# A four-layer network on one core: the pseudo-inverse recurrence with symmetric operands, and another opening of the first attention stage

## The chip, the cores and the metric

The kernel runs on one core of a Trainium2 chip. The metric is the device time of one execution in microseconds (us); lower is better. One execution is also taken by the hardware profiler, and its page and trace are what is read here. TensorE has two clock levels, 1.2 and 2.4 GHz; the profile gives the granted clock as 0.50 and 1.00 of full speed.

## The reference

The network takes x of 8 images, 16 x 16 positions and 192 channels, and applies in order: a window attention with relative positions (windows of 14 x 14, 12 heads of 16) and its MLP, a Fourier filter, a landmark attention, a mixture of experts (two of eight), a full attention and a mixture of experts (one of eight). Two places matter here. The first is the window attention:

```python
attn = jnp.einsum('bqc,bkc->bqk', q * scale, k)
attn = (attn.reshape(-1, WS, WS, WS, WS) + rel_h[:, :, :, :, None] + rel_w[:, :, :, None, :]).reshape(-1, N, N)
attn = jax.nn.softmax(attn, axis=-1)
out = attn @ v
```

The second is the pseudo-inverse in the landmark attention, on one 16 x 16 matrix per image and head:

```python
v = (1.0 / jnp.max(jnp.sum(k_mat, axis=-2), axis=-1))[:, None, None] * jnp.swapaxes(k_mat, -1, -2)
for _ in range(6):
    kv = k_mat @ v
    v = 0.25 * v @ (13.0 * I - kv @ (15.0 * I - kv @ (7.0 * I - kv)))
```

Here kv starts as K times its own transpose (times a number), which is symmetric, and each step of the recurrence is a polynomial in it.

## The kernel before

`build` (L2852) runs the layers as stages, each with its own programs for the engines: TensorE (PE), VectorE (DVE), ScalarE (ACT), GpSimd (POOL), and SyncE (SP), which issues most DMAs. An engine runs its program in order; the engines meet at semaphores. The prefix of a tile names its stage: l0a is the window attention, l2i the pseudo-inverse, l3a the full attention.

**Window attention, `window_attention` (L961).** The work is 12 groups k (pairs of images times groups of four heads), each of three parts j (two windows, then the border), each of four heads s: 36 steps n of four items, 144 items. For an item `score` (L1071) multiplies four times into one of two banks psS, and VectorE takes the maxima (`maxima`, L1267), so that the item after next waits for `max_done`. The maxima of a group are split in three bf16 pieces by POOL, turned by TensorE (`turn_max`), copied by ACT and sent by DMA as three more rows of QS. Only then can `score_t` (L1111) form the transposed scores, ACT take their exponentials (`exps`) and TensorE multiply with the values (`values`). `steps` (L1000) starts at n = -lead = -6: the scores run six steps, 24 items, ahead of the transposed scores. For these first 24 items TensorE does `score` alone, with one `turn_max` among them.

The inputs of a group lie in a ring of four slots. SP's `load` (L1019) issues 13 DMAs for a slot: RS from rd (one, 336 KB), QS from qd (six of 64 KB) and KS from kd (six of 64 KB, by `term_rows`, L954); `stack_in` of the slot counts all 13. ACT's queue first issues six small DMAs to kb (L1208), then the four window rows of RS (L1210), KOH (L1211) and Wo (L1212). VectorE waits for kb and spreads it into KP (L1264) before its first maxima. TensorE opens with six products of 512 columns on data that is there (L1184), each of them two records in the trace since the operands are f32; their result is overwritten. Then it waits for `pads_done` (KP) and all five constants on `c_in`, and in the first `score` for `stack_in`.

**Pseudo-inverse, `l2_inverse` (L1851).** Sixteen block-diagonal matrices of 96 x 96 are kept as [96, 16, 96]. A `product` (L1879) is 16 f32 matmuls (32 records), four to a PSUM bank, four banks; `done` rises once per bank. K2 is turned by TensorE and copied to K2T by ACT (L1915); VectorE scales K2 to VT (L1952) and K2T to Vm (L1954), bank by bank in turn. A loop of six iterations on each engine then does six products: A = K V (to D7 by VectorE, L1960), the transpose of A (to AT by ACT, L1919), A D7 (to D15), A D15 (to D13), V D13 (to Vm by VectorE, L1969) and its transpose (to VT by ACT, L1922). A last product with K3 gives MB. That makes 6 x 6 + 1 = 37 products. The products alternate between the banks ps0 to ps3 and ps4 to ps7.

Of the kernel before, what the change touches and what calls it, by code (L numbers as in the profile page):

```python
# [9 lines left out]
ALU = mybir.AluOpType  # L10
ACT = mybir.ActivationFunctionType
# [9 lines left out]
CH = C // 2  # L21
# [13 lines left out]
K_TERM = (0, 1, 2, 0, 1, 0)  # L35
# [161 lines left out]
KS = 33  # L197
# [763 lines left out]
def window_attention(nc, G, w_out, stats_eps):  # L961
# [7 lines left out]
    with Stage(nc, "l0a") as st:  # L969
# [27 lines left out]
        c_in, kb_in, pads_done, zeroed, x_biased = st.sems("c_in kb_in pads_done zeroed x_biased")  # L997
# [20 lines left out]
        def _(sp):  # L1018
            def load(k):  # L1019
# [6 lines left out]
                term_rows(sp, KS[slot], G["kd"], at, K_TERM, stack_in[slot])  # L1026
# [824 lines left out]
def l2_inverse(nc, G, consts):  # L1851


    with Stage(nc, "l2i") as st:
# [5 lines left out]
        K2, K2T, AT, D7, D15, D13, Vm, VT = (big(n) for n in ("K2", "K2T", "AT", "D7", "D15", "D13", "Vm", "VT"))  # L1860
        ps = [st.ps(f"ps{b}") for b in range(8)]
        c_in, sm, exp_done, col_mm, col_done, bd_done, k2t_mm, k2t_done, start_done = st.sems("c_in sm exp_done col_mm col_done bd_done k2t_mm k2t_done start_done")
        a_mm, at_mm, at_done, d7_done, b_mm, d15_done, c_mm, d13_done, v_mm, vt_mm, v_done, vt_done = st.sems(
            "a_mm at_mm at_done d7_done b_mm d15_done c_mm d13_done v_mm vt_mm v_done vt_done")
# [6 lines left out]
        ITERATIONS = 6  # L1871

# [6 lines left out]
        def product(pe, b0, lhs, rhs, gate, gate_at, done):  # L1879

            for b in range(NBK):
                for s, at in zip(gate, gate_at):
                    pe.wait_ge(s, at + b)
                for g in range(b * GB, (b + 1) * GB):
                    mm = nc.tensor.matmul(ps[b0 + b][0:CH, (g % GB) * CH:(g % GB + 1) * CH], lhs[:, g, :], rhs[:, g, :], start=True, stop=True)  # L1885
                mm.then_inc(done, 1)

        @block.tensor
        def _(pe):
            pe.wait_ge(c_in, 48)  # L1890
# [8 lines left out]
            with pe.Fori(0, ITERATIONS) as it:  # L1899

                product(pe, 0, K2T, Vm, (v_done, vt_done), (4 * it + 1, 4 * it + 1), a_mm)
                product(pe, 4, Vm, K2T, (vt_done,), (4 * it + 1,), at_mm)
                product(pe, 0, AT, D7, (at_done, d7_done), (4 * it + 1, 4 * it + 1), b_mm)
                product(pe, 4, AT, D15, (d15_done,), (4 * it + 1,), c_mm)
                product(pe, 0, VT, D13, (d13_done,), (4 * it + 1,), v_mm)
                product(pe, 4, D13, VT, (d13_done,), (4 * it + 1,), vt_mm)
            product(pe, 0, VT, K3, (v_done, vt_done), (4 * ITERATIONS + 1, 4 * ITERATIONS + 1), mb_mm)

        @block.scalar
        def _(act):  # L1910
# [5 lines left out]
            with act.Fori(0, ITERATIONS) as it:  # L1916
                for b in range(NBK):
                    act.wait_ge(at_mm, 4 * it + b + 1)
# [963 lines left out]
```

## Time and profile before

| | us |
|---|---|
| median of 3 runs | 1607.22 |
| lowest, highest of them | 1604.24, 1630.35 |
| profiled execution, its time | 1617.94 |
| profiled execution, its span | 1616.1 |
| mean granted clock in it | 0.823 |

The span reaches from the first to the last instruction; the execution's own time is 1.8 us longer. The window attention takes from 157.2 us to about 380 us of the span, the pseudo-inverse from 758.7 to 870.7 us. In the views, a group of rows gives the start and the length in us, the engine, the line and the tiles (out <- in); "PEld" is TensorE's weight load, which overlaps its matmuls; a bracket at the end of a row tells how long the engine sat idle before it and what released it.

### The profile page before, as it was taken

The numbers are of one execution on the slowest core, as the hardware profiler recorded it, in microseconds if no ns is written. First come the engines' busy times: TensorE is split into PE (matmuls) and PEld (weight loads), VectorE is DVE, ScalarE is ACT, GpSimd is POOL, SyncE is SP. The second block draws the span as 40 slices with busy tenths as digits, with TensorE's granted clock in tenths as the row PEclk, the third lists the DMA queues.
The fourth block names the chain that finished last, engine by engine and source line by source line (L and its number), as shares of the span: only waits on it lengthen the run. The fifth ranks groups of instructions, "written<-read, shape, count | busy, mean of one in ns | idle before, by whom it ended". The sixth has DMA issues, their size and how long they took to land. (4 is left out here: it accounts for less than half of the span.)

```text
span 1616.1 us, 25003 instructions
## 1 busy us (share of the span) xinstructions
PE 1212.6 (75%) x8342; PEld 968.3 (60%) x8343; DVE 604.4 (37%) x1430; ACT 468.9 (29%) x947; POOL 302.0 (19%) x513
## 2 busy tenths in 40 slices
PE   1866899996986786888997564699945679961892
PEld 0765677884974565766997453466634435541782
DVE  2333433542103654434554340233335557522011
ACT  0633133553422231333211023111103336620330
POOL 3224300112000111000001306100036531114003
PEclk9975556997996997987998756799978789965896
DMA  4223522311111001000000055111112243141453
GB/s 87 59 67 108 109 58 58 87 31 33 39 61 42 0 0 38 1 0 4 1 0 6 14 147 163 47 48 46 47 53 67 79 136 95 42 106 39 118 141 88
DMA packets 123405, 95.53 MB, mean 59 GB/s; under 512 B 33298, under 2 KB 114508, under 8 KB 123212
## 3 DMA queue, kind: packets, MB, share of 16 engines
q1 hardware_dynamic: 108648, 83.13, 19.2%
q0 software_dynamic: 4608, 9.44, 2.2%
q10 hardware_dynamic: 10084, 2.11, 0.8%
q8 instruction: 38, 0.62, 0.2%
q14 instruction: 27, 0.22, 0.0%
HBM read 67.21 MB, written 35.20 MB: 63 GB/s over the span
## 5 line engine op out<-in xcount | busy, mean ns | idle before, releaser
L2402 PE MATMUL l2e_psH<-W1T,l2e_XT 96*128 x160 | 79.2, 618 | 10.1 <-issue 5.3
L1273 DVE TENSOR_REDUCE l0a_nmax<-l0a_psS 98x2 f32<-98x392 f32 x96 | 54.2, 566 | 65.8 <-PE l0a_psS L1083 63.5
L913 DVE TENSOR_REDUCE l3a_nmax<-l3a_psS 128x2 f32<-128x512 f32 x96 | 62.3, 686 | 40.0 <-PE l3a_psS L764 40.0
L1221 ACT ACTIVATE l0a_PT<-l0a_psST 98x392 f32<-98x392 f32 x96 | 47.2, 497 | 68.0 <-PE l0a_psST L1125 67.7
L869 ACT ACTIVATE l3a_PT<-l3a_psST 128x512 f32<-128x512 f32 x96 | 54.7, 596 | 31.7 <-PE l3a_psST L794 31.2
L2435 ACT ACTIVATE l2e_H<-l2e_psH 128x512 f32<-128x512 f32 x40 | 23.9, 597 | 137.3 <-PE l2e_psH L2402 137.3
L1082 PE MATMUL l0a_psS<-l0a_KS,l0a_QS 96*98 96x196 bf16 x192 | 55.2, 319 | 5.5 <-DMA l0a_KS<-kd 5.4
L2418 PE MATMUL l2e_psY<-W2T,l2e_HT 128*128 x320 | 58.5, 326 | 0.0
L2451 DVE COPY l2e_HT<-l2e_psT 128x512 f32<-128x512 f32 x40 | 27.6, 691 | 76.5 <-PE l2e_psT L2410 76.5
L1083 PE MATMUL l0a_psS<-l0a_KOH,l0a_RS 90*98 90x196 bf16 x192 | 53.4, 309 | 0.0
L2418 PEld LDWEIGHTS l2e_psY<-W2T,l2e_HT 128*128 128x128 f32 x320 | 51.1, 190 | 0.0
L1960 DVE SCALAR_TENSOR_TENSOR l2i_D<-l2i_ps,l2i_eyes 96x384 f32<-96x384 f32 x72 | 39.9, 554 | 26.8 <-PE l2i_ps L1885 19.2
L618 PE MATMUL l0r_ps<-QF,l0r_Rbd 96*84 x256 | 39.3, 327 | 14.0 <-DVE l0r_Rbd L642 14.0
L1124 PE MATMUL l0a_psST<-l0a_QS,l0a_KS 99*98 99x196 bf16 x192 | 49.3, 291 | 0.2 <-ACT l0a_PT L1221 0.2
L1125 PE MATMUL l0a_psST<-l0a_RS,l0a_KOH 90*98 90x196 bf16 x192 | 48.9, 288 | 0.0
L2402 PEld LDWEIGHTS l2e_psH<-W1T,l2e_XT 96*128 96x128 f32 x160 | 27.9, 194 | 34.7 <-issue 34.7
L2574 PE MATMUL l3e_psH<-l3e_XT,expert_W 96*128 96x256 f32 x192 | 44.8, 395 | 4.0 <-DMA expert_b<-in_L_ffn_b 2.7
L618 PEld LDWEIGHTS l0r_ps<-QF,l0r_Rbd 96*84 96x84 f32 x256 | 39.2, 238 | 14.3 <-issue 14.3
L161 PE MATMUL l3p_psT<-ident,l3p_xn 128*96 128x128 f32 x32 | 8.0, 425 | 50.1 <-DVE l3p_xn L151 50.1
L1378 PE MATMUL l0m_psH<-l0m_xT,l0m_W 96*128 96x256 f32 x192 | 44.7, 395 | 0.4 <-ACT l0m_xT L173 0.4
L2574 PEld LDWEIGHTS l3e_psH<-l3e_XT,expert_W 96*128 96x128 f32 x192 | 37.8, 199 | 10.7 <-issue 5.2
L1082 PEld LDWEIGHTS l0a_psS<-l0a_KS,l0a_QS 96*98 96x98 bf16 x192 | 30.1, 157 | 22.8 <-issue 9.9
(485 smaller groups left out, 2979.4 us busy)
## 6 DMA issues: line engine op xcount, KB each, us to landing
expert_W<-in_L_ffn_w SPq DMA_DIRECT2D x16, 576.0 KB, 4.3
l2r_raw<-in_L_ffn_w SPq DMA_DIRECT2D x16, 384.0 KB, 4.5
l0a_QS<-qd SPq DMA_DIRECT2D x72, 64.0 KB
l0a_KS<-kd SPq DMA_DIRECT2D x72, 64.0 KB
l3a_QS<-qd SPq DMA_DIRECT2D x72, 64.0 KB, 2.3
l3a_KS<-kd SPq DMA_DIRECT2D x72, 64.0 KB, 2.3
rd<-l0r_r_p SPq DMA_DIRECT2D x24, 168.0 KB
l0a_RS<-rd SPq DMA_DIRECT2D x12, 336.0 KB
```

The source lines that it names most:

```text
L618: mm = nc.tensor.matmul(ps[bank][0:HB * WS, col + k * B * cnt:col + (k + 1) * B * cnt], Rbd[:, axis, i0 + k, :], free(src, [2 * T, B // 2] ...
L869: nc.scalar.activation(PT[n % 3][:, s, :], psST[item % 2][:, :], ACT.Exp).then_inc(exp_done, 1)
L913: nc.vector.tensor_reduce(nmax[k % 2][:, TI * u:TI * (u + 1), s], psS[item % 2][:, :].rearrange("p (t k) -> p t k", t=TI), AX.X, ALU.max, ...
L1082: nc.tensor.matmul(o, q_[:, s, q], k_[:, s, keys], start=True, stop=False)
L1083: mm = nc.tensor.matmul(o, r_[:, s, q], KOH[:, keys], start=False, stop=True)
L1124: nc.tensor.matmul(o, k_[:, s, keys], q_[:, s, q], start=True, stop=False)
L1125: mm = nc.tensor.matmul(o, KOH[:, keys], r_[:, s, q], start=False, stop=True)
L1221: ex = nc.scalar.activation(PT[n % 3][0:WQ, s, :], psST[item % 2][0:WQ, 0:2 * W0], ACT.Exp)
L1273: mx = nc.vector.tensor_reduce(nmax[k % 2][0:WQ, 2 * j:2 * (j + 1), s], psS[item % 2][0:WQ, 0:2 * W0].rearrange("p (t k) -> p t k", t=2), ...
L2402: mm = nc.tensor.matmul(psH[b][:, :], XT[b][:, k, :], G["W1T"][:, k, bass.ds(e * FI, FI)], start=(k == 0), stop=(k == 1))
L2418: mm = nc.tensor.matmul(psY[b][:, 0:C], HT[b][:, mb, :], G["W2T"][:, bass.ds(e * NM + mb, 1), :].rearrange("p a c -> p (a c)"), start=(mb ...
L2574: mm = nc.tensor.matmul(psH[k2][:, m % 2 * CAP:(m % 2 + 1) * CAP], W1[b][:, k, m * P:(m + 1) * P], XT[b][:, k, :], start=(k == 0), stop=(k ...
```

## The change

In the pseudo-inverse, the transposed product of A is dropped: since A is symmetric, A itself is used as the stationary operand. A is kept by ACT (in place of AT), and VectorE makes D7 from this copy in SBUF instead of from PSUM. In iterations 0 to 3, A of the next iteration is formed as 0.25 A D13, so that V is not needed, and only VT is carried. Iteration 4 forms V D13 and K V anew; iteration 5 forms VT alone. The loops are written out. At the start VectorE makes all four banks of Vm first, then VT.

In the window attention, the opening has 20 products instead of 6. The six KS loads of slot 0 move from SP's queue to ACT's, where they follow the window rows of slot 0 and KOH and stand ahead of kb and the other three window rows. TensorE waits before the first score for the first two constants only (`c_in` 32); for the other window rows (`rest_in`) at k = 1, and for `pads_done` at the first border item (n = 2).

```diff
@@ window_attention
-                term_rows(sp, KS[slot], G["kd"], at, K_TERM, stack_in[slot])
+                if k:
+                    term_rows(sp, KS[slot], G["kd"], at, K_TERM, stack_in[slot])
...
                     pe.wait_ge(stack_in[k % ring], 13 * 16 * (k // ring + 1))
+                    if k == 1:
+                        pe.wait_ge(rest_in, 16 * (ring - 1))
+                if j == 2 and k == 0 and s == 0:
+                    pe.wait_ge(pads_done, 1)
...
-            for c in range(6):
+            for c in range(20):
                 nc.tensor.matmul(psS[0][:, :], G["ident"][0:CH, :], G["QF"][:, 0, c * W2 % (B * T):c * W2 % (B * T) + W2], start=True, stop=True)
-            pe.wait_ge(pads_done, 1)
-            pe.wait_ge(c_in, 16 * (ring + 1))
+            pe.wait_ge(c_in, 32)
...
+            act.dma_start(RS[0][RR:RM, :, :], rows(G["consts"]["winrows"], 0, [W2, RM - RR], [0, GQ], [1, W2])).then_inc(c_in, 16)
+            act.dma_start(KOH[:, :], G["consts"]["koh"]).then_inc(c_in, 16)
+            term_rows(act, KS[0], G["kd"], 0, K_TERM, stack_in[0])
             for t, piece in enumerate(K_TERM):
                 act.dma_start(kb[t * HD:(t + 1) * HD, :], rows(G["kbd"], piece * C, [1, HD], [HD, NH]), allow_slow_non_contiguous=True).then_inc(kb_in, 16)
-            for k in range(ring):
-                act.dma_start(RS[k][RR:RM, :, :], rows(G["consts"]["winrows"], 0, [W2, RM - RR], [0, GQ], [1, W2])).then_inc(c_in, 16)
-            act.dma_start(KOH[:, :], G["consts"]["koh"]).then_inc(c_in, 16)
+            for k in range(1, ring):
+                act.dma_start(RS[k][RR:RM, :, :], rows(G["consts"]["winrows"], 0, [W2, RM - RR], [0, GQ], [1, W2])).then_inc(rest_in, 16)
@@ l2_inverse, TensorE
-            with pe.Fori(0, ITERATIONS) as it:
-
-                product(pe, 0, K2T, Vm, (v_done, vt_done), (4 * it + 1, 4 * it + 1), a_mm)
-                product(pe, 4, Vm, K2T, (vt_done,), (4 * it + 1,), at_mm)
-                product(pe, 0, AT, D7, (at_done, d7_done), (4 * it + 1, 4 * it + 1), b_mm)
-                product(pe, 4, AT, D15, (d15_done,), (4 * it + 1,), c_mm)
-                product(pe, 0, VT, D13, (d13_done,), (4 * it + 1,), v_mm)
-                product(pe, 4, D13, VT, (d13_done,), (4 * it + 1,), vt_mm)
-            product(pe, 0, VT, K3, (v_done, vt_done), (4 * ITERATIONS + 1, 4 * ITERATIONS + 1), mb_mm)
+            LO, HI = 0, 4
+            product(LO, K2T, Vm, a_mm, (v_done, 0))
+            for it in range(ITERATIONS):
+                at = NBK * it
+                product(HI, A, D7, b_mm, (d7_done, at))
+                product(LO, A, D15, c_mm, (d15_done, at), (vt_done, at))
+                if it < LAST - 1:
+                    product(HI, A, D13, a_mm, (d13_done, at))
+                    product(LO, D13, VT, vt_mm, (d13_done, at))
+                elif it == LAST - 1:
+                    product(HI, VT, D13, v_mm, (d13_done, at))
+                    product(LO, D13, VT, vt_mm, (d13_done, at))
+                    product(HI, K2T, Vm, a_mm, (v_done, NBK))
+                else:
+                    product(HI, D13, VT, vt_mm, (d13_done, at))
+            product(LO, VT, K3, mb_mm, (vt_done, NBK * ITERATIONS))
@@ l2_inverse, ScalarE and VectorE
+            keep(A, 0, a_mm, a_done, 0, 1.0)
+            for it in range(ITERATIONS):
+                at = NBK * it
+                if it < LAST - 1:
+                    keep(A, 4, a_mm, a_done, at + NBK, 0.25)
+                keep(VT, 4 if it == LAST else 0, vt_mm, vt_done, at, 0.25)
+                if it == LAST - 1:
+                    keep(A, 4, a_mm, a_done, at + NBK, 1.0)
...
+                minus(D7, lambda b: A[:, gs(b), :], 0, a_done, at, d7_done)
+                minus(D15, lambda b: bank(4 + b), 2, b_mm, at, d15_done)
+                minus(D13, bank, 1, c_mm, at, d13_done)
+                if it == LAST - 1:
+                    for b in range(NBK):
+                        dve.wait_ge(v_mm, b + 1)
+                        nc.vector.tensor_scalar(Vm[:, gs(b), :], bank(4 + b), 0.25, None, ALU.mult).then_inc(v_done, 1)
```

`keep` is four ACT copies, one per bank, each waiting for its bank of the product and raising `done`; `minus` is four VectorE operations of the same kind.

## Rows read from the trace of the kernel before

**Rows 1.** The page: TensorE's granted clock in 40 slices of the span, in tenths
```profile
PEclk9975556997996997987998756799978789965896
```

**Rows 2.** Timeline of the pseudo-inverse, one full iteration
```profile
785.57 2.80 PEld L1885 LDWEIGHTS l2i_ps<-l2i_Vm,l2i_K2T 96*96 96x96 f32 x32
...
786.54 2.59 DVE L1960 SCALAR_TENSOR_TENSOR l2i_D<-l2i_ps,l2i_eyes 96x384 f32<-96x384 f32 x4
...
789.26 0.49 ACT L1919 ACTIVATE l2i_AT<-l2i_ps 96x384 f32<-96x384 f32 x1 [2.91 <-PE l2i_ps L1885]
...
791.01 5.52 PEld L1885 LDWEIGHTS l2i_ps<-l2i_D,l2i_AT 96*96 96x96 f32 x64
```

**Rows 3.** Busy time of L1885 by stretch: us, PE, PEld, granted clock, DMA
```profile
785.50:867.10 81.60, 81.60 (x963) 81.60 (x962) 1.00 0.00 0
```

**Rows 4.** Timeline of the pseudo-inverse, its first two products and VectorE's scaling
```profile
766.07 5.25 PEld L1885 LDWEIGHTS l2i_ps<-l2i_Vm,l2i_K2T 96*96 96x96 f32 x32
...
767.89 0.55 DVE L1954 TENSOR_TENSOR l2i_Vm<-l2i_K2T,l2i_inv 96x384 f32<-96x384 f32 x1
...
771.19 3.58 PEld L1885 LDWEIGHTS l2i_ps<-l2i_K2T,l2i_Vm 96*96 96x96 f32 x32
```

**Rows 5.** By stretch, window attention: us, PE, PEld, DVE, ACT, POOL busy, clock, DMA, GB/s
```profile
203.20:270.10 66.90, 66.90 (x510) 52.39 (x509) 20.64 (x41) 20.79 (x42) 2.57 (x12) 0.50 0.20 52
...
286.50:299.00 12.50, 12.50 (x171) 9.94 (x170) 8.90 (x25) 6.70 (x14) 3.36 (x12) 1.00 0.36 93
...
327.40:377.00 49.60, 49.23 (x671) 37.93 (x669) 22.25 (x58) 28.12 (x62) 7.55 (x28) 1.00 0.09 25
```

**Rows 6.** By stretch, exponentials (tile PT, ACT) alone: us, busy and count, clock
```profile
190.20:203.20 13.00, 3.98 (x8) 0.50 0.01 2
203.20:270.10 66.90, 17.57 (x36) 0.50 0.20 52
286.50:299.00 12.50, 5.86 (x12) 1.00 0.36 93
```

**Rows 7.** Timeline of the opening of the window attention
```profile
157.22 2.88 ACTq L1208 DMA_DIRECT2D l0a_kb<-kbd  x6
...
157.26 7.67 PE L1184 MATMUL l0a_psS<-QF,ident 96*128 96x512 f32 x12 [14.56 <-PEq L72]
...
160.81 0.34 PEld L1184 LDWEIGHTS l0a_psS<-QF,ident 96*128 96x128 f32 x1 [0.52 <-issue]
...
163.91 0.19 PEld L1184 LDWEIGHTS l0a_psS<-QF,ident 96*128 96x128 f32 x1 [0.24 <-issue]
...
166.80 2.48 DVE L1264 COPY l0a_KP<-l0a_kb 96x2880 bf16<-96x2880 bf16 x1 [19.23 <-DMA l0a_kb<-kbd]
...
170.29 0.37 PE L1082 MATMUL l0a_psS<-l0a_KS,l0a_QS 96*98 96x196 bf16 x1 [5.36 <-DMA l0a_KS<-kd]
```

**Rows 8.** By stretch, the same opening; columns as in rows 5
```profile
162.90:164.90 2.00, 2.00 (x5) 0.57 (x3) 0.00 (x0) 0.00 (x0) 1.94 (x2) 1.00 1.17 132
...
166.90:170.30 3.40, 0.01 (x1) 0.04 (x2) 2.38 (x1) 0.00 (x0) 0.87 (x1) 0.76 1.10 227
170.30:183.50 13.20, 13.07 (x73) 9.86 (x73) 8.56 (x16) 0.59 (x1) 0.86 (x4) 0.50 1.01 210
```

**Rows 9.** Timeline, maxima of the first items, and the first exponential
```profile
174.36 1.22 DVE L1273 TENSOR_REDUCE l0a_nmax<-l0a_psS 98x2 f32<-98x392 f32 x2 [0.33 <-PE l0a_psS L1083]
...
178.00 0.48 DVE L1276 TENSOR_REDUCE l0a_nmax<-l0a_psS 120x1 f32<-120x312 f32 x1 [0.17 <-PE l0a_psS L1092]
...
190.35 0.50 ACT L1221 ACTIVATE l0a_PT<-l0a_psST 98x392 f32<-98x392 f32 x1 [7.47 <-PE l0a_psST L1125]
```

**Rows 10.** By stretch, the full attention; columns as in rows 5
```profile
1315.50:1319.00 3.50, 2.53 (x16) 1.05 (x15) 2.77 (x6) 1.28 (x1) 0.55 (x3) 1.00 0.44 140
...
1366.70:1370.10 3.40, 1.92 (x22) 0.86 (x20) 2.18 (x4) 1.74 (x3) 1.39 (x7) 1.00 0.30 84
1370.20:1373.50 3.30, 3.30 (x21) 1.58 (x19) 1.62 (x3) 1.57 (x3) 0.00 (x0) 0.50 0.24 72
```

More of the change, by code:

```diff
@@ L996, in window_attention @@
         o_turned, ot_done, y_full, x_added, w_in, ident_done, ones_done = st.sems("o_turned ot_done y_full x_added w_in ident_done ones_done")
-        c_in, kb_in, pads_done, zeroed, x_biased = st.sems("c_in kb_in pads_done zeroed x_biased")
+        c_in, rest_in, kb_in, pads_done, zeroed, x_biased = st.sems("c_in rest_in kb_in pads_done zeroed x_biased")
         block = st.block()
@@ L1871, in l2_inverse @@
         ITERATIONS = 6
+        LAST = ITERATIONS - 1
         @block.sync
@@ L1877, in _, with product @@
             sp.dma_start(eyes[:], consts["eyes"]).then_inc(c_in, 16)
[L1879 to L1886, printed above, removed]
         @block.tensor
         def _(pe):
+            def product(b0, lhs, rhs, done, *gates):
+                for b in range(NBK):
+                    for s, at in gates:
+                        pe.wait_ge(s, at + b + 1)
+                    for g in range(b * GB, (b + 1) * GB):
+                        mm = nc.tensor.matmul(ps[b0 + b][0:CH, (g % GB) * CH:(g % GB + 1) * CH], lhs[:, g, :], rhs[:, g, :], start=True, stop=True)
+                    mm.then_inc(done, 1)
             pe.wait_ge(c_in, 48)
@@ L1915, in _, with keep @@
                 nc.scalar.activation(K2T[:, gs(b), :], bank(4 + b), ACT.Copy).then_inc(k2t_done, 1)
-            with act.Fori(0, ITERATIONS) as it:
+            def keep(dst, b0, mm, done, at, scale):
                 for b in range(NBK):
-                    act.wait_ge(at_mm, 4 * it + b + 1)
-                    nc.scalar.activation(AT[:, gs(b), :], bank(4 + b), ACT.Copy).then_inc(at_done, 1)
-                for b in range(NBK):
-                    act.wait_ge(vt_mm, 4 * it + b + 1)
-                    nc.scalar.activation(VT[:, gs(b), :], bank(4 + b), ACT.Copy, scale=0.25).then_inc(vt_done, 1)
+                    act.wait_ge(mm, at + b + 1)
+                    nc.scalar.activation(dst[:, gs(b), :], bank(b0 + b), ACT.Copy, scale=scale).then_inc(done, 1)
+            keep(A, 0, a_mm, a_done, 0, 1.0)
[6 more added lines that the diff above has]
+                    keep(A, 4, a_mm, a_done, at + NBK, 1.0)
             for b in range(2):
@@ L1949, in _, with minus @@
             dve.wait_ge(bd_done, 1)
+            scale = lambda b: free(inv[:, b * GB:b * GB + 1], [1, GB], [0, CH])
             for b in range(NBK):
[L1951 to L1952 removed]
                 dve.wait_ge(k2t_done, b + 1)
[L1954 to L1956 removed]
+                nc.vector.tensor_tensor(Vm[:, gs(b), :], K2T[:, gs(b), :], scale(b), ALU.mult).then_inc(v_done, 1)
+            for b in range(NBK):
+                nc.vector.tensor_tensor(VT[:, gs(b), :], K2[:, gs(b), :], scale(b), ALU.mult).then_inc(vt_done, 1)
+            def minus(dst, src, k, gate, at, done):
                 for b in range(NBK):
[L1959 to L1969 removed]
+                    dve.wait_ge(gate, at + b + 1)
+                    nc.vector.scalar_tensor_tensor(dst[:, gs(b), :], src(b), -1.0, free(eyes[:, k, 0:1], [0, GB], [1, CH]), ALU.mult, ALU.add).then_inc(done, 1)
+            for it in range(ITERATIONS):
+                at = NBK * it
+                minus(D7, lambda b: A[:, gs(b), :], 0, a_done, at, d7_done)
+                minus(D15, lambda b: bank(4 + b), 2, b_mm, at, d15_done)
+                minus(D13, bank, 1, c_mm, at, d13_done)
+                if it == LAST - 1:
+                    for b in range(NBK):
+                        dve.wait_ge(v_mm, b + 1)
+                        nc.vector.tensor_scalar(Vm[:, gs(b), :], bank(4 + b), 0.25, None, ALU.mult).then_inc(v_done, 1)
             for b in range(2, NBK):
```

22 lines of the change are left out of this document (4 added, 18 removed).

## The prediction

> **What bounds the kernel now.** I read the page first, for TensorE's granted clock in slices [rows 1], since both places of the change are TensorE's. Slices 5 to 7 of 40 (160 to 280 us) stand at 8, 5 and 5 tenths: most of the first half of the window attention goes at the low level, 1.2 GHz. Slices 21 and 22, the pseudo-inverse, stand at 9: nearly all of it has 2.4 GHz. Then I read each place by stretch.
>
> *Pseudo-inverse.* From 785.5 to 867.1 TensorE is busy for all of its 81.60 us [rows 3]. Those are five iterations of six products, so a product costs 81.60 / 30 = 2.72 us and a bank 0.68 us. The next reader starts 0.97 us after a product's first load (785.57 to 786.54 for VectorE; the ACT copy stands the same way to its product), and copies take 0.49 us on ACT, four VectorE operations 2.59 us [rows 2]. All of it fits beside the next product. TensorE alone bounds this place.
>
> *Window attention.* From 203.2 to 270.1 TensorE is busy 66.90 of 66.90 us at 0.50; from 286.5 to 299.0 it is busy 12.50 of 12.50 at 1.00 [rows 5]. The same work runs in both: the exponentials count 36 items in 66.9 us (1.86 each) against 12 in 12.5 (1.04 each) [rows 6]. TensorE bounds both and the clock decides. The opening shows how the low clock came. The six products end at 164.9 us, already at 1.00 [rows 7, 8]; then TensorE waits 5.4 us, for KP and last for the inputs of slot 0 [rows 7]; in that wait the clock falls (0.76 in its last 3.4 us), and the scores from 170.3 on run at 0.50 [rows 8].
>
> **The pseudo-inverse.** New products: 1 for the first A; 4 in each of iterations 0 to 3; 5 in iteration 4; 3 in iteration 5; 1 for MB. That is 1 + 16 + 5 + 3 + 1 = 26 against 37, 11 fewer. Is it still bound by TensorE? The tightest link is a product whose operand VectorE makes from the product right before: 0.97 us to VectorE's start, 0.55 us for a bank, so the first bank is there 1.52 us after the start, under 2.72. A to D7 now goes over ACT and then VectorE: 0.97 + 0.49 + 0.55 = 2.0 us, under 2.72 in iteration 5 (where b follows A directly) and with VT's product between them elsewhere. VectorE has 12 operations of 0.65 us (2.59 / 4), 7.8 us, in an iteration of 4 x 2.72 = 10.9; ACT eight of 0.49. If these links took double they would cost some tenths per iteration, 0 to 6 us in all. I take nothing.
> The first products ran at the low clock (loads of 5.25 and 3.58 us [rows 4]); that stretch is the same time in both kernels, and what is removed are products at the full level. VectorE's new order ends Vm earlier (before it ended at 768.4 [rows 4]) and delays VT, which is needed two products later: nothing. The written-out loops: the window attention is written out too and gets its instructions at 171 matmul records in 12.5 us [rows 5], here 963 in 81.6 [rows 3]: 13.7 against 11.8 a microsecond, so code supply has cover. Term: 11 x 2.72 = **-29.9 us** (bounds -24 to -31).
> The Trainium skill, Runtime: NRT & Kernel Launch, section "Instruction fetch mechanics", says that a taken branch may have to fetch its target before going on, and advises to unroll. By that rule writing out would give something more; in rows 3 no time is idle over five turns of the loop, so the trace shows nothing to give back, and I add nothing.
>
> **The opening.** Twenty products are 40 records. At the low clock one took 0.34 + 0.52 = 0.86 us, at the full one 0.19 + 0.24 = 0.43 [rows 7]. The twelve ended at 164.9; 28 more at 0.43 make 12.0: **176.9 us**, 6.6 later than the first score now.
> Is the rest there by then? ACT issues the window rows of slot 0, KOH, six KS, then six kb, at 0.48 each (2.88 / 6 [rows 7]): KS by 161.1, kb by 164. SP has six DMAs fewer ahead of slot 1. All DMA queues together are saturated in both kernels until 183.5 (share 1.0 to 1.17 [rows 8]), so bytes set the time: slot 0 landed at 170.2, with its last KS issued as SP's 13th, at 157.2 + 13 x 0.48 = 163.5; issued 2.4 us earlier it should land at 165 to 170. kb landed 6.7 us after its last issue (160.1 to 166.8); now it stands behind KS, 164 + 6.7 = 171, up to 175 with the fuller queue. VectorE needs 2.48 us for KP before its first maximum: 173.5 to 177.5. So TensorE goes from the last product into the first score with no gap, or one under 1 us. The wait for `pads_done` comes 8 items later and costs nothing. Behind the wait for `rest_in` at k = 1 stand scores that need slot 1 anyway.
>
> **The clock, where I must choose.** Now the scores start at 1.00. The 24 items before the first transposed score are then bound by the ring of two banks: 0.33 us of matmuls, half of the 0.66 now, some 0.2 to VectorE, 0.57 for the maximum, 0.05 back [rows 9], for two items 1.15 to 1.2. That is 0.6 an item, 0.53 for the eight border items (0.48 [rows 9]): 16 x 0.6 + 8 x 0.53 = 13.8 us, against 19 now. First exponential at 176.9 + 13.8 + 1 = 191.7, against 190.35 [rows 9]: **+1.4**. In these 14 us TensorE streams only some 54% of the time. Does the clock stay? The nearest rows are the full attention's: it kept 1.00 over 3.5 us with 16 records of bf16 scores (busy 2.53), and lost it after a stretch busy 1.92 of 3.40 [rows 10], which holds one idle of 1.5 us. Mine lies between: its gaps are short (0.3 us) but frequent. From item 25 on, nothing is open: the same work kept 1.00 to the end of the stage once it had it, with TensorE busy 49.23 of 49.60 us at the end [rows 5]. I take that it stays, since no gap comes near 1.5 us.
> The page TensorE: Matmul & The Clock Gate of the Trainium skill, table "Why this matters for your kernels", says that continuous work brings the full clock and only idle gaps lose it. On staying, that is my case and gives the same sum. On rising it disagrees with rows 5: 66.9 us of continuous work never brought it. By the page the stage would have been at full level anyway and this part would cost +6.6; the measurement decides.
> If it stays, 44 items (8 + 36 [rows 6]) run at the full rate: before 13.0 + 66.9 = 79.9 us; now 36 x 1.04 = 37.5 for the 36, and the first eight scaled alike (13.0 x 37.5 / 66.9) 7.3, in all 44.8: **-35.1**. With the later start: -33.7.
>
> **Sum.** Against the profiled execution: 1617.9 - 29.9 - 33.7 = 1554.3. That execution is 10.7 over the median, 1607.2. If it lost these by a later return of the clock in this very attention, the new kernel has no such loss and 1554 stands; if elsewhere, 1543.5. I take **1550**.
>
> **Rivals.**
> *R1, the clock falls during the 24 lead items.* For it: streaming 54% of the time, near the stretch that lost it; VectorE may still be at KP at 177. Against: no long gap. Then the opening is pure delay: if it falls half way, 12 items at 0.6 and 12 at 0.79 (19 / 24) are 16.7 us, 176.9 + 16.7 + 1 = 194.6, +4.2, and the low stretch is as before. 1617.9 - 29.9 + 4.2 = 1592, less up to 10.7 against the median: 1581 to 1592.
> *R2, it falls and stays down.* The clock returned at 271 us before without a visible cause, so it might not return in this stage. The work from 270.1 to 377.0, 106.9 us at full level, then takes 1.78 times as long (66.9 / 37.5), +83: 1592 + 83 = 1675. It decides from 15 / 0.78 = 19 us of such work on; past that the kernel is slower than the median.
> *R3, the attention gains in part:* the clock is lost and comes back tens of microseconds earlier than 271: each gives 0.44 us, 1560 to 1580.
> *R4, the recurrence does not do what it says:* links over ACT and VectorE show up as waits. At most 6 us, so 1556; it is inside the range.
>
> **Chances.** Forecast (with R4) 0.67, R1 0.21, R3 0.08, R2 0.04. The range takes the forecast's own 1540 to 1562 and reaches over R3 to most of R1; below it leaves room for a shorter lead: 1537 to 1590. Within 2% of 1607.2, about what a measurement of this kernel can tell from no change, is 1575 to 1639. Faster by over 2%: forecast and most of R3, 0.73. Same: R1 and the rest of R3, 0.24. Slower: R2, 0.03.
>
> **What would show it.** Right: records of the opening end near 177 and the first score follows within 1 us; granted clock 1.00 from 163 us to the end of the attention; first exponential near 192; stage end some 34 us earlier; 26 products, 2.72 us each, with no idle TensorE between them, the first at half rate. Wrong: a clock of 0.50 in the stretch 177 to 191 (R1), first maxima waiting for KP, or idle TensorE before a product in the recurrence (R4).

## The result and the profile after

| | before | after |
|---|---|---|
| median, lowest and highest, us | 1608.03 (1601.51 to 1635.07, 20 runs) | **1589.86** (1579.57 to 1614.76, 20 runs) |
| ratio, 95% interval | 1 | 0.988 (0.986 to 0.991) |
| profiled execution: time, span | 1617.94, 1616.1 | 1590.27, 1588.4 |
| mean granted clock in it | 0.823 | 0.827 |

The kernel gained 18 us by the medians, 1.2% by the ratio. The ratios leave out the executions that were over 1.5% above the fastest of their kernel, medians and ranges leave out none. The forecast was 1550, a gain of 57; the time came out where rival R1 had it (1581 to 1592). The profiled executions say where the 27.7 us between their spans are. The pseudo-inverse took 81.5 us (758.2 to 839.7) in place of 111.4, the window attention 226.0 (160.2 to 386.2) in place of 230.8, and it started 3.0 us later, in stages ahead of it that the change does not touch. The stages between the two took 1.4 us more and those behind them 2.8, also untouched. (The lengths of a stage end here, in every run alike, with the start of its last or nearly last instruction, at most 0.6 us before the last result is there.)

The page: the granted clock in 40 slices of the profile after, beside [rows 1].

```profile
PEclk9975757998997997888897655999977799965896
```

Slices 5 to 7 (159 to 278 us) still stand at 7, 5 and 7 tenths, where they stood at 5, 5 and 6 before: most of the low stretch in the attention has stayed. The pseudo-inverse now lies in slice 20, slice 21 and the start of 22 (from 754 us on), which stand at 8, 9 and 7.

**The pseudo-inverse.** The timeline of TensorE's weight loads in the profile after, its start and its end, beside [rows 2, 4]:

```profile
765.52 5.25 PEld L1899 LDWEIGHTS l2i_ps<-l2i_Vm,l2i_K2T 96*96 96x96 f32 x32
...
770.64 9.05 PEld L1899 LDWEIGHTS l2i_ps<-l2i_D,l2i_A 96*96 96x96 f32 x96
...
779.61 2.80 PEld L1899 LDWEIGHTS l2i_ps<-l2i_VT,l2i_D 96*96 96x96 f32 x32
...
825.85 2.80 PEld L1899 LDWEIGHTS l2i_ps<-l2i_Vm,l2i_K2T 96*96 96x96 f32 x32
828.57 5.52 PEld L1899 LDWEIGHTS l2i_ps<-l2i_D,l2i_A 96*96 96x96 f32 x64
834.01 2.80 PEld L1899 LDWEIGHTS l2i_ps<-l2i_VT,l2i_D 96*96 96x96 f32 x32
```

Each group starts where the one ahead of it has its last bank: 825.85 to 828.57 is one product, 2.72 us, and 828.57 to 834.01 two, 5.44. No row carries a bracket for idle time. Busy time of L1899 in a stretch from the second product on, beside [rows 3] (us; PE, PEld; clock, DMA):

```profile
774.00:838.60 64.60, 64.60 (x762) 64.60 (x761) 1.00 0.01 2
```

TensorE is busy for all of 64.60 us, so the links over ScalarE and VectorE cost nothing. The first product is at the low level as before (5.25 us).

**The opening of the attention.** Timeline, beside [rows 7, 9]:

```profile
160.22 19.68 PE L1189 MATMUL l0a_psS<-QF,ident 96*128 96x512 f32 x40 [14.35 <-PEq L72]
...
175.65 1.66 DVE L1270 COPY l0a_KP<-l0a_kb 96x2880 bf16<-96x2880 bf16 x1 [24.92 <-DMA l0a_kb<-kbd]
...
180.35 1.04 DVE L1279 TENSOR_REDUCE l0a_nmax<-l0a_psS 98x2 f32<-98x392 f32 x2 [3.04 <-PE l0a_psS L1088]
...
182.18 0.29 PE L1087 MATMUL l0a_psS<-l0a_KS,l0a_QS 96*98 96x196 bf16 x1 [0.19 <-DVE l0a_nmax L1279]
...
184.68 0.23 PE L1094 MATMUL l0a_psS<-l0a_KS,l0a_QS 96*120 96x120 bf16 x1 [0.28 <-DVE l0a_nmax L1279]
...
198.18 0.50 ACT L1227 ACTIVATE l0a_PT<-l0a_psST 98x392 f32<-98x392 f32 x1 [7.47 <-PE l0a_psST L1130]
```

The 40 records of the opening end at 179.9, 19.7 us after the start of the stage, KP is ready in time, and the first score follows with no gap. Then TensorE waits for VectorE's maxima, 0.2 to 0.4 us at a time by the matmuls. By stretch (us; PE, PEld, DVE, ACT, POOL; clock, DMA, GB/s), beside [rows 5, 8]:

```profile
164.80:179.70 14.90, 14.90 (x36) 6.50 (x35) 1.66 (x1) 0.31 (x1) 5.82 (x3) 1.00 1.12 180
179.70:185.30 5.60, 4.55 (x40) 3.21 (x39) 4.28 (x9) 0.00 (x0) 0.00 (x0) 1.00 1.04 212
185.30:198.20 12.90, 12.57 (x75) 9.63 (x74) 8.83 (x17) 0.60 (x2) 1.50 (x7) 0.50 0.08 19
198.20:257.00 58.80, 58.80 (x439) 46.77 (x441) 19.08 (x37) 19.07 (x39) 8.60 (x10) 0.50 0.16 40
257.00:386.00 129.00, 122.33 (x1580) 97.58 (x1572) 61.26 (x146) 64.64 (x137) 16.46 (x62) 1.00 0.21 55
```

This is where most of the missing 35 us are. The lead items began at 1.00, as forecast; 5.6 us later, at 185.3, with the ninth of 24 maxima under way, the clock fell to 0.50 with no long gap anywhere, and came back at 257.0, after 34 exponentials (before: after 45, at 271.1).

### The profile page after: what moved, and what is told of

Read it like the earlier page. It is cut to its first block and busy times, and to the rows that moved or that the text cites. A ratio compares the mean times of both kernels' runs of the same rounds, so it can differ in the third digit from the quotient of the medians.

```text
span 1588.4 us, 24173 instructions
## 1 busy us (share of the span) xinstructions
PE 1188.7 (75%) x8018; PEld 936.3 (59%) x8019; DVE 592.1 (37%) x1410; ACT 469.3 (30%) x947; POOL 302.9 (19%) x513
## 5 line engine op out<-in xcount | busy, mean ns | idle before, releaser
L2479 DVE COPY l2e_HT<-l2e_psT 128x512 f32<-128x512 f32 x40 | 27.7, 692 | 78.4 <-PE l2e_psT L2438 78.3
L1087 PE MATMUL l0a_psS<-l0a_KS,l0a_QS 96*98 96x196 bf16 x192 | 51.1, 300 | 0.9 <-DVE l0a_nmax L1279 0.8
L1088 PE MATMUL l0a_psS<-l0a_KOH,l0a_RS 90*98 90x196 bf16 x192 | 49.1, 288 | 0.0
L1899 PE MATMUL l2i_ps<-l2i_D,l2i_A 96*96 96x96 f32 x512 | 45.2, 250 | 0.0
L1899 PEld LDWEIGHTS l2i_ps<-l2i_D,l2i_A 96*96 96x96 f32 x512 | 44.8, 167 | 0.0
```

Source lines behind the costliest of these rows:

```text
L1087: nc.tensor.matmul(o, q_[:, s, q], k_[:, s, keys], start=True, stop=False)
L1088: mm = nc.tensor.matmul(o, r_[:, s, q], KOH[:, keys], start=False, stop=True)
```

## The experiments

Four theories were open. A: the recurrence gives its 29.9 us whole; the opening only delays the first scores, since its lead items are too thin to hold the clock. B: the recurrence gives less than it seems to. C: the new order of the loads costs time, or bounds the start. D: the clock falls for another reason than the thin lead. In this kernel the times of one version spread over some 30 us where the clock has been lost, so medians are given with their range. Where the times of a version fall in two groups (opening_only and early_start), each group is read by itself. Every execution also has its mean granted clock over the whole span, profiled or not, and that tells whether the clock was held in the attention: it was 0.811 to 0.832 in the 20 executions of the changed kernel, and is 0.842 to 0.845 in lead_fill below, which holds it.

### Each part by itself

*inverse_only*: the kernel before, with the new `l2_inverse` (the edit in short).

```diff
 def window_attention(...):      # as before
-def l2_inverse(...):            # old
+def l2_inverse(...):            # new
```

> The kernel before with the new pseudo-inverse alone; the window attention is untouched. Theory A (the recurrence gives all it can, the opening takes some back): 11 products of 2.72 us fewer, so 29.9 us under the kernel before, ratio 0.981, and the pseudo-inverse from its first to its last instruction 81.5 us long as against 111.4. Theory B (the recurrence gives only what the changed kernel showed, 18 us, because stages behind it lose some, and the opening is neutral): ratio 0.989.

Measured: 1587.55 us (1579.56 to 1602.82, 6 runs; before on the same chip 1611.71), ratio 0.985 (0.980 to 0.991). The pseudo-inverse took 79.8 us. The interval holds both A's 0.981 and B's 0.989, so the times alone don't decide between them.

*opening_only*: the changed kernel with the old `l2_inverse`.

> The kernel before with the new opening alone; the pseudo-inverse is the old one. Theory A: the clock falls among the 24 lead items as in the changed kernel (it did at 185.3 us), so the later first score is pure delay: some 7 to 12 us over the kernel before, ratio 1.004 to 1.008. Theory B (neutral opening): 1.000. If the clock stays in some executions and not in others, the times fall in two groups 35 us apart.

Measured: 1617.75 us (1589.25 to 1647.49, 12 runs), 6.0 over the median of before, but in two groups, as the expectation allowed. Ten executions stand from 1610.72 to 1647.49, with a mean granted clock of 0.813 to 0.833; their median is 1621.2, 9.5 over before, which is A's price. Two stand at 1589.25 and 1591.04 with 0.844, which is lead_fill's clock: by that, and by their time, 21 to 22 us under before, the clock held through the lead in these two without any fill. Neither was profiled. The profiled execution is one of the longer ones (1641.07). Its stretches, columns as above:

```profile
166.30:190.00 23.70, 21.94 (x94) 11.31 (x93) 8.43 (x15) 0.31 (x1) 7.07 (x8) 1.00 0.98 176
190.20:295.80 105.60, 105.41 (x775) 83.71 (x774) 36.03 (x71) 31.43 (x63) 10.96 (x21) 0.50 0.17 45
```

The clock fell within the lead here too, at 190.1, and stayed down over 105 us, until 53 exponentials were done. In inverse_only it was also 53, in the profile of before 45, in that of after 34. So the return varies from profile to profile; at some 0.8 us an item lost, that alone is 15 us between 34 and 53. The times of one kernel spread the same way: of the changed kernel's 20 executions the shortest (1579.57) has a mean granted clock of 0.832 and the longest (1614.76) of 0.812. Theory A holds: the recurrence is worth 24 us by the medians on the old opening, 28 on the new one (1617.75 to 1589.86), 29.9 by its own stage, and no stage behind it was found to give it back. B is not excluded by the times of inverse_only; it falls by the profiles, this one's stage and lead_fill's whole sum below. The opening alone costs 9.5 us in ten executions of twelve.

*six_products*: the changed kernel with 6 products in the opening, but the new order of the loads.

```diff
-            for c in range(20):
+            for c in range(6):
```

> The changed kernel with 6 opening products again, and its new order of loads and waits. Theory A: the 14 more products (28 records of 0.43 us, 12 us) are what costs; without them the first score waits for data and starts about 9 us earlier than in the changed kernel, at the low clock. The time is that of inverse_only within some us, ratio to the kernel before 0.979 to 0.983. Theory C (the new order of loads costs, by kb and KP coming late): no better than the changed kernel, 0.988.

Measured: 1587.81 us (1581.07 to 1602.79, 6 runs), ratio 0.986 (0.981 to 0.992). Timeline of the opening:

```profile
165.97 0.26 PE L1087 MATMUL l0a_psS<-l0a_KS,l0a_QS 96*98 96x196 bf16 x1 [1.17 <-DMA l0a_KS<-kd]
...
171.78 1.66 DVE L1270 COPY l0a_KP<-l0a_kb 96x2880 bf16<-96x2880 bf16 x1 [24.38 <-DMA l0a_kb<-kbd]
...
173.96 0.40 PE L1087 MATMUL l0a_psS<-l0a_KS,l0a_QS 96*98 96x196 bf16 x1 [7.13 <-DVE l0a_nmax L1279]
```

The new order brings slot 0 early, 9 us after the start of the stage (157.0), where it took 13 before. But two scores later everything waits 7.13 us for VectorE, which waits for kb, now 14.8 us after the start. The load order trades one wait for another, at no cost (C falls for the changed kernel), and the low clock covers the rest. Six products or twenty, the medians are 2 us apart (1587.81 and 1589.86), in favour of six: with the clock lost in either case, the other fourteen buy nothing. Like inverse_only, the run stands a little above the ratio of 0.979 to 0.983 that A gave it.

### Holding the clock through the lead

*lead_fill*: the changed kernel; TensorE does one more product of 128 stationary columns by 512 behind each of the 24 lead scores, into a bank that is overwritten later.

```diff
+            def fill(n):
+                k = n // J % ring
+                nc.tensor.matmul(psST[0][:, :], KS[k][0:SR, 0, 0:P], QS[k][0:SR, 0, :], start=True, stop=True)
...
                     score(n + lead, s)
+                    if n < 0:
+                        fill(n + lead)
```

> The changed kernel with one more matmul behind each of the 24 lead scores (bf16, 128 columns wide, 512 columns streamed, 0.22 us at the full clock; its result is overwritten). A lead item then streams 0.55 us of about 0.6. Theory A (the clock falls because the lead items stream about half of the time, 98 columns wide): granted clock 1.00 through the lead and on to the end of the attention, and the 34 us of the prediction come: ratio to the kernel before 0.958 to 0.965. Theory D (the clock falls in the lead for another reason, for instance the kind of matmul or the mere length of the stretch): it falls all the same, and the time is that of the changed kernel or 1 to 3 us more, ratio 0.988 to 0.991.

Measured: **1558.72 us** (1554.73 to 1564.71, 5 runs), ratio 0.968 (0.964 to 0.973); once more on another chip (lead_fill_again, below) 1562.26. By stretch:

```profile
165.60:180.30 14.70, 14.70 (x40) 6.65 (x39) 1.66 (x1) 0.31 (x1) 4.30 (x2) 1.00 1.10 191
180.30:195.20 14.90, 14.90 (x132) 10.10 (x131) 13.11 (x25) 0.59 (x1) 1.18 (x6) 1.00 0.32 66
195.20:356.60 161.40, 155.10 (x2015) 124.01 (x2013) 80.40 (x184) 83.18 (x175) 25.04 (x74) 1.00 0.22 59
```

The ratio is a little above the 0.958 to 0.965 that was expected. The clock is at 1.00 from 165.6 to within 1 us of the end of the attention. In the lead TensorE is busy 14.90 of 14.90 us (ends of matmuls are modelled, so small gaps don't show), against 4.55 of 5.60 without the fill. The stage takes 197.7 us, 33.1 less than before, where the prediction had 33.7 for this term. The fill costs the lead next to nothing: 14.9 us from the first maximum to the first exponential, 0.62 us an item against the 0.60 of the unfilled lead while it was at 1.00, since VectorE sets the pace (13.11 busy). The range of the times shrinks from 35 us (20 runs) to 10 (5 runs) with it, and the other 12 executions of sixteen_fill and split_spread below stay within 8: most of the spread had been the return of the clock. D falls.

*narrow_fill*: the same with 32 stationary columns.

```diff
-                nc.tensor.matmul(psST[0][:, :], KS[k][0:SR, 0, 0:P], QS[k][0:SR, 0, :], start=True, stop=True)
+                nc.tensor.matmul(psST[0][0:32, :], KS[k][0:SR, 0, 0:32], QS[k][0:SR, 0, :], start=True, stop=True)
```

> The filled kernel (the changed kernel plus one product behind each of the 24 lead scores, 1558.7 us), with the fill product of 32 stationary columns instead of 128; it streams the same 512 columns, so TensorE is busy as long. If the time for which TensorE streams holds the clock, nothing changes: clock 1.00 through the window attention, 1555 to 1565 us. If it is how much of the array works, the fill counts for a quarter: the clock falls in the lead items as it did at 185.3 us without a fill, the attention takes some 226 us instead of 198, and the time is 1585 to 1595 us. My choice: it stays, 1560, chance 0.6.

Measured: 1565.95 us (1561.03 to 1570.5, 4 runs), ratio 0.973 (0.968 to 0.977). Lead and the rest of the stage:

```profile
178.40:197.50 19.10, 19.10 (x131) 10.67 (x131) 13.25 (x25) 0.59 (x1) 1.28 (x6) 1.00 0.23 50
197.50:357.80 160.30, 155.10 (x2016) 124.04 (x2013) 80.42 (x184) 83.04 (x175) 24.05 (x69) 1.00 0.23 59
```

The clock holds with a fill of 32 stationary columns as with one of 128. But the lead takes 19.1 us in place of 14.9, although as many columns are streamed. The timeline shows where:

```profile
180.46 0.25 PE L1088 MATMUL l0a_psS<-l0a_KOH,l0a_RS 90*98 90x196 bf16 x1
180.63 0.39 PE L1102 MATMUL l0a_psST<-l0a_QS,l0a_KS 96*32 96x512 bf16 x1
180.95 0.29 PE L1087 MATMUL l0a_psS<-l0a_KS,l0a_QS 96*98 96x196 bf16 x1
```

The narrow product starts 0.17 us after the score ahead of it and the next score 0.32 after the narrow product; in lead_fill these steps are 0.09 and 0.22 (score at 179.97, fill at 180.06, next score at 180.28). An item is 0.79 us in place of 0.62. Going to a 32-column product and back cost 0.17 us.

### Are the twenty products needed?

*old_opening_fill*: inverse_only with the fill; the opening as before.

> The kernel before with the new pseudo-inverse and the fill products in the 24 lead items, but the opening as it was: six products, all KS by SP's queue. The wait of 5.4 us before the first score remains, and in it the clock falls. Theory A says the fill alone doesn't help here unless it also brings the clock back; the filled lead at the low level costs up to 24 x 0.4 = 10 us more than the unfilled one. If the low clock only returns where it did (near 271 us), the time is 1587 (the kernel before with the new pseudo-inverse) plus 0 to 10: 1587 to 1597. If 24 items of nearly unbroken work bring it back, it returns within the lead, the attention is 25 to 30 us shorter, and the time is 1555 to 1565: then the twenty products and the new load order were not needed. I give the first 0.6.

Measured: 1585.82 us (1576.53 to 1597.46, 6 runs), ratio 0.985 (0.980 to 0.990). The first score and the stretches:

```profile
175.47 0.37 PE L1082 MATMUL l0a_psS<-l0a_KS,l0a_QS 96*98 96x196 bf16 x1 [4.99 <-DMA l0a_KS<-kd]
```

```profile
174.40:202.60 28.20, 27.13 (x135) 21.21 (x136) 13.89 (x26) 0.62 (x2) 1.85 (x9) 0.50 0.51 108
202.60:239.00 36.40, 36.40 (x270) 29.29 (x272) 12.01 (x23) 12.02 (x25) 7.34 (x5) 0.50 0.12 33
```

The clock fell in the wait of 4.99 us, and a filled lead, busy 27.13 of 28.20, did not bring it back; TensorE stood at 0.50 for another 36.4 us busy without a break. The time is that of inverse_only. So by the medians the opening without the fill is worth nothing, the fill without the opening nothing, and the two together 29 us (1587.55 to 1558.72); opening_only says that the opening alone holds the clock now and then (2 of 12), and in none of the changed kernel's 20.

*early_start*: lead_fill with 12 products, and kb ahead of KS in ScalarE's queue.

```diff
-            for c in range(20):
+            for c in range(12):
...
-            term_rows(act, KS[0], G["kd"], 0, K_TERM, stack_in[0])
             for t, piece in enumerate(K_TERM):
                 ...
+            term_rows(act, KS[0], G["kd"], 0, K_TERM, stack_in[0])
```

> The filled kernel with 12 products in the opening instead of 20 and the six kb loads ahead of the six KS loads of slot 0 in ScalarE's queue. Twelve products end 8 x 0.43 = 3.4 us plus what 20 of them took beyond (28 records at 0.43) earlier: about 170 instead of 177 to 180 us. kb should land by 168 and be spread by 170, KS of slot 0 by 170. Theory A (only the cover of TensorE decides): first maximum near 171 instead of 180.3, clock held at 1.00, stage 6 to 9 us shorter than the filled kernel's 197.7, time 1550 to 1553. Rival C (the transfers bound the start: they are saturated until about 183): slot 0 or slot 1 lands late, TensorE idles over a microsecond before or among the lead scores, the gain is under 3 us, and if the clock falls there the time is 1585 or more.

Measured: 1594.81 us at the median, but in two groups: 1551.73, 1557.24 and 1557.40, and four from 1594.81 to 1602.15. The profiled execution (1599.07) is of the second:

```profile
174.12 1.88 PE L1193 MATMUL l0a_psS<-QF,ident 96*128 96x512 f32 x4
177.77 0.26 PE L1087 MATMUL l0a_psS<-l0a_KS,l0a_QS 96*98 96x196 bf16 x1 [1.78 <-DMA l0a_KS<-kd]
```

```profile
178.10:204.60 26.50, 26.50 (x134) 20.48 (x132) 13.52 (x25) 0.59 (x1) 1.77 (x9) 0.50 0.44 94
204.60:263.30 58.70, 58.70 (x440) 46.77 (x442) 19.07 (x37) 18.91 (x39) 8.29 (x9) 0.50 0.15 40
```

Slot 0 came 1.78 us late, the clock was at 0.50 from 178.0 on, and the lead took 26.1 us in place of 14.9. The quick group is the one in which the clock held: its mean granted clock is 0.842 to 0.846, that of the other four 0.818 to 0.820. That the slot came in time there is what these rows suggest; no profile of a quick execution was taken. Rival C is real for an opening this short: by these rows the lateness of one transfer decides over some 40 us. The gain of 6 to 9 us that A had expected didn't come in the quick group either: its median, 1557.24, is 1.5 under lead_fill's.

*sixteen_fill* (lead_fill with 16 products) and *split_spread* (14 products; VectorE spreads KP for four heads before item 6 and for the other eight before item 16, in place of all before its first maximum) look for a shorter opening that is safe:

```diff
@@ split_spread
-            dve.wait_ge(kb_in, 16 * len(K_TERM))
-            nc.vector.tensor_copy(KP[0:SR, :, :], free(kb[:, 0:1], [1, NH], [0, 2 * PKP])).then_inc(pads_done, 1)
...
+                    if (n + lead, s) == (1, 2):
+                        dve.wait_ge(kb_in, 16 * len(K_TERM))
+                        spread(0, GQ)
+                    if (n + lead, s) == (4, 0):
+                        spread(GQ, NH)
                     maxima(n + lead, s)
```

> The filled kernel once more, on the chip of the next two, as their measure: all theories give 1555 to 1565 us.

> The filled kernel with 16 products in the opening instead of 20. They end 8 x 0.43 = 3.4 us earlier, 17.2 us after the stage's start; KP was ready 16.5 us after it (175.97 against 159.44), slot 0 well before. Theory A (TensorE must have no gap, and then a lead that is full): the clock holds, first maximum 17 to 17.5 us after the start instead of 20.9, time 3 to 3.5 us under the filled kernel's, 1555. Rival C (the transfers vary from run to run, and 20 products were their cover): in some executions KP is later than the products, TensorE idles over a microsecond after two scores and the clock falls, so that some times stand at 1590 and more beside others at 1555. I give the first 0.7.

> The filled kernel with 14 products, and with the spreading of kb into KP cut in two by heads and moved behind the first maxima (four heads before item 6, eight before item 16), where the border items first need it. The products end 12 x 0.43 = 5.2 us earlier, 15.3 us after the stage's start, and kb (14.9 us after it in the filled kernel) is needed only some 4 us later still. VectorE's 1.66 us for KP move from before the first maximum into the lead, where VectorE sets the pace: they are paid there. Net 5.2 - 1.7 = 3.5 us gain over the filled kernel, at less risk from a late kb than with sixteen products: 1555, with the clock held. Rival C: slot 0 or slot 1 lands late, the clock falls in some executions, and these stand at 1585 to 1600. I give the first 0.65.

Measured on one chip: lead_fill_again 1562.26 (1558.81 to 1563.31), sixteen_fill 1560.70 (1558.90 to 1564.47), split_spread 1561.59 (1559.66 to 1566.06), 6 runs each; ratios 0.967, 0.967 and 0.968, each within 0.005. The clock held in all 18, by their times and mean granted clocks (0.836 to 0.844), and in the three profiles. The stage was shorter as expected, 194.3 and 193.1 us against 198.1, but of these 4 and 5 us only 1.6 and 0.7 are in the medians, less than their spread: in the profile of sixteen_fill the pseudo-inverse starts 0.1 us earlier than in that of lead_fill_again, though the attention ended 4.0 earlier. What takes it up is the clock again, in the stages between: they took 375.1 us at a mean granted clock of 0.86 in sixteen_fill (356.6 to 731.7) and 371.2 at 0.87 in lead_fill_again (360.6 to 731.8), which is 102.4 and 95.1 us at the low level. Over the thirteen profiles of all runs this untouched part takes from 368.6 to 375.2 us, mostly the more the longer it is at the low level (85.7 to 102.4 us). A gain of 4 us ahead of it is below what a few runs can show. In sixteen_fill TensorE waited once, at kb's late arrival:

```profile
179.99 0.29 PE L1087 MATMUL l0a_psS<-l0a_KS,l0a_QS 96*98 96x196 bf16 x1 [1.19 <-DVE l0a_nmax L1285]
```

and kept its clock over it, after two filled items and ahead of 22 more.

### The evidence from the full attention

The prediction had taken the full attention's scores as its nearest row for a clock that stays [rows 10]. They were not what I took them for. Timeline of the kernel before, out of that very stretch:

```profile
1315.91 0.39 PE L764 MATMUL l3a_psS<-l3a_KS,l3a_QS 96*128 96x256 bf16 x2
1316.14 0.38 PE L771 MATMUL l3a_psST<-l3a_QS,l3a_KS 96*128 96x512 bf16 x1
1316.50 0.39 PE L764 MATMUL l3a_psS<-l3a_KS,l3a_QS 96*128 96x256 bf16 x2
1316.73 0.38 PE L771 MATMUL l3a_psST<-l3a_QS,l3a_KS 96*128 96x512 bf16 x1
```

L771 is a fill product: the kernel before already had 16 of them in the lead of its full attention, and none in that of the window attention. *full_no_fill* is lead_fill without these 16.

```diff
                 if scored(n):
                     score(n + lead, s)
-                    if n < 0:
-                        fill(n + lead)
```

> The filled kernel with the fill products of the full attention taken out (16 of them, which were there in the kernel before too). This tests the evidence that I used: the stretch of bf16 scores that kept 1.00 in the full attention had fill products among its scores. If thin lead items lose the clock there as in the window attention, it falls within the lead of the full attention, and that stage is 10 to 40 us longer: 1570 to 1600. If the full attention keeps its clock without them, they were no part of the reason: 1555 to 1563. I give the first 0.65.

Measured: 1569.56 us (1563.33 to 1574.06, 4 runs), ratio 0.973 (0.968 to 0.977): 7 to 11 over lead_fill's two medians. By stretch, its lead and what follows:

```profile
1256.90:1259.30 2.40, 1.42 (x9) 0.37 (x7) 2.27 (x4) 0.00 (x0) 0.00 (x0) 1.00 0.46 142
1259.50:1279.80 20.30, 19.05 (x94) 8.04 (x94) 14.78 (x23) 8.24 (x13) 2.52 (x12) 0.50 0.34 102
```

TensorE was busy 1.42 of 2.40 us in the first lead items, and at 1259.4 the clock fell, for 20 us. The stage took 135.6 us, 33 of them at the low level, against 128.0 and 131.1, 9 and 15 at the low level, in the two profiles of lead_fill. The fall is the same as in the window attention, at a second place. Its price is less sure: the stage varies from 127.9 to 134.6 us over the other twelve profiles, all with its fill, and the medians put it at the low end of what was expected (10 to 40) or under it, because the clock came back sooner.

## Why the prediction was wrong

- *The pseudo-inverse, 11 products of 2.72 us, -29.9.* Right in every step: 111.4 to 81.5 us is 29.9, products 2.72 us apart, no idle time, the first at half rate. R4 did not happen. The medians give 24 and 28, within the spread that the clock's return makes.
- *The end of the opening and KP.* Right: 40 records ended 19.7 us after the start of the stage, the forecast had 176.9 - 157.2 = 19.7; with the stage's start 3 us later that is 179.9. KP was ready at 177.3, the first score came with no gap. What I had not reckoned with is that this is close: in sixteen_fill KP was the last to come, in early_start slot 0.
- *The pace of the lead.* Right while the clock lasted: two items each 1.20 us (180.35, 181.56, 182.76, 183.97), 0.60 an item. First maximum to first exponential took 17.8 us, against 13.8 + 1 at full clock and 14.9 measured in lead_fill.
- **The step that failed: "I take that it stays, since no gap comes near 1.5 us".** Staying was made a matter of the longest gap, and the runs speak otherwise. Up to the fall at 185.3 the lead items had single idles of TensorE of at most 0.39 us by the matmuls, 0.60 by the weight loads. sixteen_fill keeps the clock over 1.19 us by the matmuls, 1.55 by the weight loads. The longest of the changed kernel, then the one of sixteen_fill:

```profile
180.97 0.12 PEld L1087 LDWEIGHTS l0a_psS<-l0a_KS,l0a_QS 96*98 96x98 bf16 x1 [0.60 <-DVE l0a_nmax L1279]
179.98 0.12 PEld L1087 LDWEIGHTS l0a_psS<-l0a_KS,l0a_QS 96*98 96x98 bf16 x1 [1.55 <-DVE l0a_nmax L1285]
```

  lead_fill still has idles in its weight loads (0.15 to 0.32 us) and keeps it. What differs is the work between the gaps, which the fill adds. The nearest row was read without its lines: 4 of the 16 records in [rows 10] were fill products, and the scores there without them lose the clock too (full_no_fill). The fall is not certain either: by the mean granted clocks it came in 20 of 20 executions of the changed kernel, in 10 of 12 of opening_only.
- *What the clock is worth, -33.7 with the later start.* Right, and proved by the fill: 230.8 to 197.7 us is -33.1. The whole sum then stands as well: the profiled spans of before and lead_fill differ by 1616.1 - 1552.8 = 63.3, where the prediction had 29.9 + 33.7 = 63.6. That it meets so closely is in part chance: the pseudo-inverse gave 31.6 there, since fewer of its first products ran at the low level, and the rest of the span took 1.5 back. Against the medians it is 1611.71 - 1558.72 = 53.0: the profiled execution of before lay 6 us above its median there, that of lead_fill 4 under its own. With the clock held, the kernel is still 9 us over the forecast of 1550, and my 4 us for the profiled execution were too few.
- *R1* was the case that came: 1581 to 1592 was its price, 1589.86 the result. It had the clock fall half way; it fell at the ninth of 24. I had given it 0.21, on the argument of the gap. That its time fits so well is luck in part: it had the attention 4.2 us longer, and the profile has it 4.8 shorter, since the clock came back after 34 exponentials and not 45; the later start (3.0) and the untouched stages (4.2) made up for that.
- *A misreading.* In [rows 1] slices 5 to 7 stand at 5, 5 and 6, not at 8, 5 and 5, and the pseudo-inverse is in slices 20 to 22, at 9, 9 and 8. The sum uses the stretches, not the slices, so no term of it changes.

The Trainium skill has the rule that would have spoken for R1, beside the one I weighed. TensorE: Matmul & The Clock Gate, section "A second HAM failure mode: psum-queue depth-cycling", describes a kernel in which TensorE idles so briefly and so often between groups of products, as it cycles through PSUM banks, that the clock moves between its two levels. The trace agrees on the fall: two banks in turn, idles of 0.2 to 0.4 us, the clock lost at 185.3. It does not agree on the return: no burst brought it back for 71.7 us, of which TensorE was busy 71.4 (12.57 + 58.80).

What stays open is the return. With the clock lost, it came after 22 to 53 exponentials in the seven profiles that lost it (old_opening_fill 22, six_products 33, after and early_start 34, before 45, inverse_only and opening_only 53), and TensorE was busy nearly throughout. But the places are not arbitrary. In all seven the return came shortly after TensorE had turned f32 data of 128 rows by products with the identity. In five of them these were the four products that turn a group's sums, which end 1.7 to 2.5 us before it; they come once in twelve items, and that is why the counts lie 11 or 12 apart. In the other two they were the eight that turn the first pair's output, which end 0.3 and 1.0 us before it. The first row is of after (return at 257.0), the other two of inverse_only (return at 289.0):

```profile
253.43 1.12 PE L1164 MATMUL l0a_psO<-ident,l0a_sums 128*128 128x128 f32 x4
286.80 1.06 PE L1169 MATMUL l0a_psA<-ident,l0a_O 128*96 128x128 f32 x4
287.65 1.06 PE L1169 MATMUL l0a_psB<-ident,l0a_O 128*96 128x128 f32 x4
```

The same products also ran at the low clock without a return: in before at 223.3 and 245.6 us, and only the third time, at 267.9, did it follow; in inverse_only three times. Whether they bring the clock back, or only stand where it happens to come, no run here tests; a run that puts such products into the low stretch earlier would.

## What to carry to other kernels

Where TensorE waits in turn for a slower engine before a long dense stretch, count what it does there, not only how long its longest gap is, and if the clock could go, put a product that nobody reads behind each item: here 24 products of 0.22 us, in the shadow of VectorE, kept the clock, which was worth 33 us in the stage. Here such a fill and a start without a long wait paid only together; test a change of this kind with both. Look at the mean granted clock of every execution, not of the profiled one alone: it showed two quick executions of opening_only that the median hides. And before a row is used as the nearest one, read the lines and tiles of its records: mine held the very fill that the case at hand lacked.

## What the runs showed of the hardware that was not expected

- TensorE lost its full clock while it was busy 4.55 of 5.60 us, and then stood at 0.50 for up to 105.6 us in which it was busy 105.41 (opening_only). Once at 1.00, the filled lead and the same work after it kept it for 190 us (sixteen_fill: busy 182.40 of 190.90).
- A filled lead holds the clock (14.90 of 14.90 us busy) but does not fetch it back (27.13 of 28.20, then 36.40 of 36.40, at 0.50).
- In all seven profiles that lost it, the clock came back within 2.6 us after f32 products of 128 rows with the identity; such products also ran up to three times without a return.
- A product of 32 stationary columns between products of 98 cost 0.17 us an item more than one of 128, with the same 512 columns streamed.
- The transfers of the opening moved by about a microsecond from one profile to the next: with the same order of loads kb was spread from 14.8 us (six_products), 15.4 (after) and 16.0 (sixteen_fill) after the start of the stage.
